# Two turns of a rotating PSUM schedule are moved in an attention and feed-forward kernel

## The reference

```python
q, k, v = x @ Wq.T, x @ Wk.T, x @ Wv.T          # x: layer norm of the input
# 4 query groups x 8 heads of 16 features; k and v have 8 heads
scores = einsum('bsqhd,bthd->bqhst', qh, kh) * 16 ** -0.5
a_dot = einsum('bqhst,bthd->bsqhd', softmax(scores), vh)
sigma_q = elu(q)                                  # by query group, 128 features
a_mem = sigma_q @ memory / (sigma_q @ memory_norm)
w = sigmoid(memory_weight)
x = x_in + a_dot * (1 - w) + a_mem * w
# second layer
x_fp8 = clip(layernorm(x) / s, -448, 448).astype(float8_e4m3fn)
out = x + (x_fp8 * s) @ (weight * weight_scale).T
```

## Time and profile before

| what | value |
|---|---|
| median of three runs | 1954.8 us |
| profiled execution | 1954.8 us |
| its span, first to last instruction | 1952.7 us |
| ACT busy | 1848.2 us, 95% |
| PE busy | 1726.5 us, 88% |
| DVE busy | 1621.5 us, 83% |
| granted TensorE clock | 1.000 |

### The profile page before, as it was taken

How to read it: one execution, slowest core, us unless ns; L and a number is a source line. 1 busy time by engine, 2 the same in 40 slices (tenths; PEclk the granted TensorE clock), 3 DMA queues, 4 the chain that set the end, 5 groups by cost and what they waited for, 6 DMA issues and landing times.

```text
span 1952.7 us, 77800 instructions
## 1 busy us (share of the span) xinstructions
PE 1726.5 (88%) x35876; PEld 674.2 (35%) x35876; DVE 1621.5 (83%) x1893; ACT 1848.2 (95%) x2069; POOL 102.2 (5%) x150
## 2 busy tenths in 40 slices
PE   9999888888888888888888888888888888888888
PEld 7884222323223322333222232232223223332235
DVE  7675789888898889888888889888888898888975
ACT  5557999999999999999999999999999999999997
POOL 5541000000000000000000000000000000000000
PEclk9999999999999999999999999999999999999999
DMA  6564111121111221121111221121112211222111
GB/s 228 195 202 130 52 52 46 36 55 55 43 45 46 77 54 45 43 76 55 43 40 52 76 55 37 51 71 48 49 43 55 76 47 41 55 60 59 42 44 46
DMA packets 131183, 127.98 MB, mean 66 GB/s; under 512 B 30451, under 2 KB 106455, under 8 KB 130855
## 3 DMA queue, kind: packets, MB, share of 16 engines
q1 hardware_dynamic: 129847, 121.15, 21.1%
q10 hardware_dynamic: 1008, 1.84, 0.3%
HBM read 86.96 MB, written 32.24 MB: 61 GB/s over the span
## 4 chain that ended last, share of the span: by engine, by line
ACT 66%; PE 28%; issue 2%; SPq 1%; DMA 1%; DVE 1%; POOL 1%; PEld 0%; PEldq 0%; ACTq 0%; DVEq 0%; POOLq 0%
ACT pool L872 65%; PE ps L1154 10%; PE ps L1038 7%; PE ps L953 6%; PE ps L1201 2%; ACT pool L881 1%; PE ps L1188 1%; DMA q_st<-guard 1%; PE ps L926 1%; SPq L542 0%; DVE late L1578 0%; SPq L541 0%; DMA resid<-in_x 0%; POOL q_sq L730 0%; SPq L545 0%
## 5 line engine op out<-in xcount | busy, mean ns | idle before, releaser
L872 ACT ACTIVATE pool<-ps 128x1024 f32<-128x1024 f32 x1861 | 1724.6, 1115 | 16.5 <-PE ps L1038 9.5
L1154 PE MATMUL ps<-pool,v_st 64*32 64x512 f32 (+1 forms) x16128 | 1043.9, 583 | 22.7 <-issue 22.7
L1038 PE MATMUL ps<-q_st,k_st 51*32 51x512 f16 x16128 | 773.3, 381 | 181.4 <-ACT pool L872 173.1
L1038 PEld LDWEIGHTS ps<-q_st,k_st 51*32 51x32 f16 x16128 | 231.8, 90 | 1029.3 <-ACT pool L872 858.1
L1154 PEld LDWEIGHTS ps<-pool,v_st 64*32 64x32 f32 x16128 | 289.9, 106 | 132.7 <-issue 53.2
L1578 DVE TENSOR_SCALAR late<-ps 128x1024 int32<-128x1024 f32 x155 | 189.7, 1225 | 80.6 <-PE ps L1038 76.7
L1594 DVE SCALAR_TENSOR_TENSOR v_tiles<-late 128x2048 f32<-128x2048 f32 (+1 forms) x93 | 180.1, 1937 | 7.7
L1596 DVE SCALAR_TENSOR_TENSOR v_tiles<-v_tiles,late 128x2048 f32<-128x2048 f32 (+1 forms) x93 | 180.1, 1936 | 3.2
L1589 DVE SCALAR_TENSOR_TENSOR late<-late 128x2048 f32<-128x2048 f32 (+1 forms) x93 | 179.4, 1929 | 0.0
L1598 DVE SCALAR_TENSOR_TENSOR pool<-v_tiles,late 128x2048 f32<-128x2048 f32 x62 | 142.1, 2292 | 2.1
L1629 DVE STREAM_TRANSPOSE by_token<-ps 128x512 f32<-128x512 f32 x126 | 82.8, 695 | 63.0 <-PE ps L1154 63.0
(11 more groups left out here) (172 smaller groups left out, 1042.0 us busy)
## 6 DMA issues: line engine op xcount, KB each, us to landing
v_st<-v_aug SPq DMA_DIRECT2D x64, 256.0 KB, 3.0
q_st<-q_aug SPq DMA_DIRECT2D x127, 128.0 KB
k_st<-k_aug SPq DMA_DIRECT2D x127, 128.0 KB
sigma_kept<-y_out SPq DMA_DIRECT2D x32, 256.0 KB, 2.0
q_aug<-parts SPq DMA_DIRECT2D x32, 256.0 KB, 2.8
wqT<-sigma_kept SPq DMA_DIRECT2D x32, 256.0 KB, 3.1
q_st<-q_aug SPq DMA_DIRECT2D x127, 64.0 KB
k_st<-k_aug SPq DMA_DIRECT2D x127, 64.0 KB
```

The source lines that it names most:

```text
L872: act.activation(held[:, half_u * 2 * CH:half_u * 2 * CH + 2 * CH], sc[slot_of("exp", unit)].rearrange("p a b -> p (a b)"), ACT.Exp, bias= ...
L1038: last = pe.matmul(dst[VW * c:VW * c + VW, x, :], k_st[RT * x:RT * x + AUG, par, keys:keys + VW], q_st[RT * x:RT * x + AUG, par, q * CH:q ...
L1154: last = pe.matmul(acc[r][VW * c:VW * c + VW, :].rearrange("v (i s) -> v i s", s=VW)[:, places, :], v_st[rows, n % 2, j, :], by_place[rows ...
```

## The change

The third strip of an odd head is scored ahead of unit 22 and no longer ahead of unit 24. The product of a tile moves from unit 1 of an odd head to unit 1 of the even head before it: tile i from head 2i + 11 to head 2i + 10, for the 26 tiles 0 to 25. Tile 26 stays in head 62. DVE's `ffn_out` moves with it, as `head` asks `product_tile` too. `slot_turns` and the tensor block ask for the memory product separately, so that an even head can have both.

```diff
--- before.py
+++ after.py
@@ -65,7 +65,7 @@
 LAST_RING = 2 * RING
 
 
-LATE_AT = ((11, 12), (8, 9, 24))
+LATE_AT = ((11, 12), (8, 9, 22))
 MEMORY_AT = 7
 WEIGHT_TURN_AT = 15
 PRODUCT_AT = 1
@@ -94,7 +94,7 @@
 
 def product_tile(n):
     tile = n // 2 - FIRST_PRODUCT_PAIR - 1
-    return tile if (n % 2 == 1 or n == LAST_HEAD - 1) and tile >= 0 else None
+    return tile if n % 2 == 0 and tile >= 0 else None
 
 
 def slot_turns(n):
@@ -105,11 +105,12 @@
         if n == LAST_HEAD:
             if a == LAST_PRODUCT_AT:
                 turns.append(("product", (NG - 1) * TPC - 1))
-        elif a == PRODUCT_AT and product_tile(n) is not None:
-            turns.append(("product", product_tile(n)))
-        elif n % 2 == 0 and a == MEMORY_AT:
-            turns.append(("memory", n // 2))
-        elif n == 2 * WEIGHT_PAIR + 1 and a == WEIGHT_TURN_AT:
+        elif n % 2 == 0:
+            if a == PRODUCT_AT and product_tile(n) is not None:
+                turns.append(("product", product_tile(n)))
+            if a == MEMORY_AT:
+                turns.append(("memory", n // 2))
+        elif n // 2 == WEIGHT_PAIR and a == WEIGHT_TURN_AT:
             turns.append(("weight", 0))
         turns.append(("exp", EXP_BASE[n] + a))
     return turns
@@ -1218,11 +1219,12 @@
                 for a in range(exp_units(n)):
                     if a in late_at(n):
                         late_scored(n + 1, late_at(n).index(a))
-                    if a == PRODUCT_AT and product_tile(n) is not None:
-                        ffn_product(product_tile(n))
-                    elif n % 2 == 0 and a == MEMORY_AT:
-                        memory_products(n // 2)
-                    elif n == 2 * WEIGHT_PAIR + 1 and a == WEIGHT_TURN_AT:
+                    if n % 2 == 0:
+                        if a == PRODUCT_AT and product_tile(n) is not None:
+                            ffn_product(product_tile(n))
+                        if a == MEMORY_AT:
+                            memory_products(n // 2)
+                    elif n // 2 == WEIGHT_PAIR and a == WEIGHT_TURN_AT:
                         turn_ffn_weight()
                     scores(n, n % 2, a)
                     if EXP_BASE[n] + a in WEIGH_AT:
```

## The result

The changed kernel takes 2005.7 us (median of 4 runs, 2002.26 to 2009.8) against 1954.9 us (4 runs): ratio 1.0259, 95% interval 1.0235 to 1.0281. It is slower by 50.8 us where +41 was forecast. The 2005.7 us lie 3.7 us above the forecast's own range (1989 to 2002 us) and 0.7 us above its range for 8 in 10 (1983 to 2005 us). The profiled execution took 2002.8 us, 48.0 more than that of before.

What follows compares the result with a forecast made beforehand. ACT, 95% busy mostly with exponentials, was taken to bound the kernel. 1954.8 + 30.1 (strip) - 9.6 (product leaves odd heads) + 20.5 (enters even heads) + 0.5 (loads) = 1996.3 us; own range 1989 to 2002, 8 in 10 1983 to 2005.

Steps and rivals of the forecast that it cites:

- The strip: Third strip ahead of unit 22 in odd heads: units 24 and 25 become late, 0.97 us in 31 heads, +30.1 us.
- The product leaves the odd heads: Odd heads without a product: each of 26 gives back 0.37 us, -9.6 us, with 0.5 us allowed for operand loads.
- Those loads are close: Start of odd heads: PE asks sooner for the next head's operands; 0 to 3 us in all, 0.5 taken.
- The transfers don't matter: Turning DMAs on SP: a tile's turning is issued more than 15 us ahead of the product, so no cost.
- A late first strip costs little, though, since the chain starts with the second strip: First strip of odd heads: a late one costs little; the allowance was 0 to 3 us, 0.5 taken.
- The product enters the even heads: Start of 26 more even heads: unit 7 loses 0.74 us and unit 1 0.05, 0.79 a head, +20.5 us.
- Rival 1: Third strip of odd heads costs nothing because DVE reaches it in time: 1966 us, chance 0.06.
- rival 2: Product in even heads costs only its odd-head price, as the delay at unit 24 lets PE catch up: 1985 us, chance 0.11.
- rival 3: Product finds room in even heads and the strip's place is harmless; only the 9.6 us gain remains: 1945 us, chance 0.04.
- Rival 4: Late strips ahead of even heads' units 11 and 12 cost another 0.3 us in 26 heads: 2004 us, chance 0.11.
- The outcome near 1983 us: ACT's exponentials spaced 0.95 us by the skill page, the strip costing about 17 us: near 1983 us, chance under 0.01.

Runs made afterwards that it cites:

- strip only: The kernel before the change, with only the odd heads' third strip moved from unit 24 to unit 22: 1984.7 us, ratio 1.0148.
- turn late: Changed kernel with the third strip back ahead of unit 24 and the turning DMAs held until ten units of the odd head are scored: 1967.3 us, ratio 1.0049.
- fill, turn late: Changed kernel with zero matmuls filling PE's gap ahead of unit 24 and the turning DMAs held until ten units are scored: 1998.0 us, ratio 1.0207.
- product only: Changed kernel with the third strip back ahead of unit 24, so only the product is moved: 1974.4 us, ratio 1.0100.
- The fill alone: Changed kernel with 48 matmuls of zeros on PE ahead of unit 24 of odd heads from 9 on: 2003.0 us, ratio 1.0246.

## Why the prediction was wrong, and where it was right

**The strip: right.** +30.1 us forecast; 0.81 a head with a product, 0.99 without (strip only), 30.9 us between "turn late" and "fill, turn late". What carried it was to take DVE's 13.03 us from the trace and to ask only when the slot is free. That it costs nothing ahead of unit 23 fits the same sum, which gives 0.81 - 0.917, below zero.

**The product leaves the odd heads: right in the heads, wrong in what it uncovers.** The 0.37 a head came back. The step that failed is "Those loads are close: [...] I allow 0 to 3 us in all and take 0.5", and with it "The transfers don't matter". I looked at the turning DMAs only as something that the product waits for, and found 15 us of room. They also stand right behind the next head's loads on SP's queue. The reason given for a small term, "A late first strip costs little, though, since the chain starts with the second strip", was wrong too. The wait holds PE, which has both strips and units 8 and 9 in one order, so ACT pays at these units at once, before DVE's chain matters: 1.4 us in head 19 of "product only". The measured term is 9 us in medians (product only is 19.3 us above its before, with the turning moved away 10.1), 8.5 against 0.5 us in the two profiles. In the profile of the changed kernel it is about 4 us, since the delay at unit 24 gives some of it back: a head that is late already waits less there (0.37 us and not 0.72 in head 19). The cue was in the profile of before: PE's five waits for the guard rows, which I had named, and PEld's twelve with 9.9 us, which I hadn't.

**The product enters the even heads: right.** 0.90 us of idle ahead of unit 7 (0.91 in head 62), 27.93 us an even head and not 27.13: 0.80 for 0.79. One head of the trace that already had the new order was worth more than any reasoning on slots.

**The clock: missing.** No term stood for it, and this is the second step that failed: the idle time ahead of unit 24 was priced as waiting alone. The forecast had the gap of PE ahead of unit 24 in its own numbers (the unit starts after 441.66 + 0.07, while the one before is issued near 440) and did not ask what idle time does to PE's speed. Two to three falls at 1.2 us are some 3 us in the profile. The unprofiled runs at a granted clock of 0.993 to 0.995 took 2004 to 2010 us, the one at 0.998 took 2002.3, so the spread goes with this term. An estimate: a mean of 0.993 over 2005 us is 28 us at half speed, about eight falls of 3.5 us, so the slower runs had more falls than the profile shows.

**Smaller ones.** Head 0 took 0.9 us more in this profile; from its first exponential to its last it takes 30.3 to 34.0 us in the profiles here, also with changes that don't touch it, and counts as noise.

**The rivals.** Rival 1 falls by "strip only", rival 2 by the 0.80 in the even heads, rival 3 by both. Rival 4 gives 2004 us and is nearest in number, but by a mechanism that isn't there: with the product in, ACT's units 12 and 13 follow as before (1.03 and 1.08 us). A right number is no proof of a mechanism. The outcome near 1983 us, worked out in the prediction by the figures of the Trainium skill, "ScalarE: Activation LUTs", did not come: ACT's spacing of 0.917 holds after the change too.

**What stays open.** The fill alone is not told from the changed kernel by its time. How a fetch packet, the turning and the guard rows hold each other up inside the DMA engines isn't shown, only that the loss needs the first two together. The clock's part is told from counts in profiles, not from a time: no run has the turning held back and the gap left unfilled. Why head 7 takes 0.9 us more than the pattern, in the changed kernel and in "fill, turn late" alike, was not followed up (0.4 us of it stand in "product only" and in before too).

## What to carry to other kernels

Where engines work in order through a ring of slots, price a move by the end of the reader that frees the slot: until that end passes the moment of need, distance costs nothing; beyond it the sum charges every unit its full time (tested for one unit here; two units further the falls of the clock are mixed in). Ask of a removed piece of work what it was hiding: take the small waits that are there already (here PE's five and PEld's twelve on the guard rows) as a sign that they can grow. Give a gap that a change makes on TensorE a price of its own, beside the wait, and keep bulk transfers away from the loads that the next stage starts with.

## What the runs showed of the hardware

- An idle gap of 1.45 us on PE, in a kernel where PE is busy 87% of the time, was followed by the clock's fall to 1.2 GHz in 2 of 31 odd heads (in "strip only", with gaps of 1.28 us in most heads and 1.97 in one, 3 of 31); one of 3.0 to 3.8 us in every odd head. With the gap filled none of 54 had one. A fall seen here lasted some 3.5 or 7 us, and the shorter cost ACT 1.2 us. The granted clock was 0.5 or 1.0 in every record.
- Issues on SP that last 0.95 to 2.0 us where their like take 0.4 to 0.6 go with a fetch of instructions (queue 8, one packet of 0.02 MB): in "product only" 31 of 34 such loads have a packet that starts in them or up to 0.4 us ahead. About as many packets (26) fall on loads that are not lengthened.
- Guard rows reached their user 1.3 us later in head 19 when transposing DMAs were issued right behind them and a fetch packet came 4.2 to 5.5 us into the head; with the transposes issued 4 to 5 us later such packets cost 0.06 us at most. 80 more instructions early in the program moved the most hurt heads from 19, 23, 27 and 31 to 37, 41, 45 and 49 and left the sum as it was (8.5 and 8.9 us).
- 48 small matmuls of zeros filled a gap on PE at 31 ns each (1.48 us) and moved no unit behind them.
